# Sliding-window attention on one core: head order across banks, and value products one clip later

## What is computed

```python
h0 = the 125 x 128 tokens of a clip; x = layernorm(h0)
qkv = (x @ W_qkv + b_qkv).reshape(B, S, 3, HEADS, HD)      # S = 125
q, k, v = ...                                              # per head
scores[s, o] = q[s] . k[s + o] * scale    for o in -32..32, inside the clip
attn = softmax(scores) @ v(shifted)
z = attn @ W_proj + b_proj + h0
out = z + (z - mean(z)) / sqrt(var(z) + 1e-5)              # per token
```

## Time and profile before

| what | value |
|---|---|
| runs | median 547.76 us (547.48 to 548.02, 3 runs) |
| the profiled execution | 550.68 us, its span 548.9 us |
| busy over the span | PE 92%, DVE 74%, ACT 65%, POOL 60% |
| 420 to 450 us (window loop) | PE 28.99 of 30 us, DVE 26.90, ACT 25.55, POOL 17.50, granted clock 1.00 |
| 400 to 410 us | PE 9.48 of 10 us, granted clock 0.75 |
| 540 us to the end | PE 1.74 of 9 us |

### The profile page before, as it was taken

How to read it: one execution, slowest core, us unless ns; L and a number is a source line. 1 busy time by engine, 2 the same in 40 slices (tenths; PEclk the granted TensorE clock), 3 DMA queues, 4 the chain that set the end, 5 groups by cost and what they waited for, 6 DMA issues and landing times.

```text
span 548.9 us, 13987 instructions
## 1 busy us (share of the span) xinstructions
PE 503.3 (92%) x4554; PEld 355.3 (65%) x4554; DVE 408.9 (74%) x1728; ACT 358.4 (65%) x1072; POOL 329.2 (60%) x367
## 2 busy tenths in 40 slices
PE   6998899999998599999999999997599999999983
PEld 4778666666665357766667776655367766776762
DVE  3797757888886367787877777865369988898993
ACT  5985558889887244454455445453578888888881
POOL 2860647778886556776666676663126555565654
PEclk9999559999999699999999999999779999999997
DMA  4440212222222010000000000000000000000000
GB/s 163 138 161 11 64 34 51 56 62 62 63 60 75 20 37 20 19 20 22 35 22 20 19 20 20 1 1 1 0 2 2 20 21 20 13 11 21 20 21 20
DMA packets 21946, 19.89 MB, mean 36 GB/s; under 512 B 14210, under 2 KB 18466, under 8 KB 21746
## 3 DMA queue, kind: packets, MB, share of 16 engines
q1 hardware_dynamic: 21298, 18.28, 11.6%
q10 hardware_dynamic: 576, 0.71, 0.4%
HBM read 16.81 MB, written 2.18 MB: 35 GB/s over the span
## 4 chain that ended last, share of the span: by engine, by line
PE 44%; DVE 15%; issue 4%; ACT 2%; POOL 2%; POOLq 0%; DVEq 0%; ACTq 0%
PE quad L802 10%; PE quad L779 9%; PE bank L824 6%; PE bank L888 4%; PE bank L899 4%; DVE quad L1156 4%; PE bank L905 3%; PE quad L771 2%; PE bank L880 2%; DVE z_all L1186 2%; DVE otok L1168 2%; DVE st_all L1188 2%; DVE wmax L1156 2%; PE bank L793 1%; PE bank L817 1%
## 5 line engine op out<-in xcount | busy, mean ns | idle before, releaser
L476 POOL TENSOR_SCALAR put<-keyb,c 100x1000 f32<-100x1000 bf16 x32 | 89.0, 2782 | 47.9 <-DMA keyb<-key_scratch 26.3
L972 ACT ACTIVATE wprobs<-quad,wmax 125x125 f32<-125x125 f32 x256 | 75.5, 372 | 19.7 <-DVE wmax L1156 19.7
L1156 DVE CUSTOM_DVE_ANT_0 quad<-quad,c 125x125 f32<-125x125 f32 x256 | 66.1, 311 | 9.1 <-PE quad L847 9.1
L609 ACT ACTIVATE probs<-quad,negmax 100x250 f32<-100x250 f32 x128 | 58.3, 467 | 21.8 <-DVE negmax L561 20.9
L779 PE MATMUL quad<-h1T,w 128*128 128x500 f32 x128 | 61.9, 609 | 0.7 <-ACT hid L943 0.6
L802 PE MATMUL quad<-w,hid 128*125 128x128 f32 x512 | 58.8, 273 | 0.1
L802 PEld LDWEIGHTS quad<-w,hid 128*125 128x125 f32 x512 | 57.3, 188 | 0.8 <-issue 0.5
L1058 POOL TENSOR_TENSOR kbd<-wkT,c 128x250 f32<-128x250 f32 x32 | 19.2, 600 | 53.0 <-ACT wkT L980 53.0
L491 PE MATMUL bank<-c,probs 100*125 100x100 f32 x256 | 48.3, 316 | 2.2 <-ACT probs L609 1.4
L491 PEld LDWEIGHTS bank<-c,probs 100*125 100x125 f32 x256 | 36.8, 209 | 20.6 <-issue 13.2
L943 ACT ACTIVATE hid<-quad,vec_cols 128x500 f32<-128x500 f32 x64 | 43.0, 675 | 7.4 <-PE quad L779 4.1
(11 more groups left out here) (131 smaller groups left out, 1267.9 us busy)
## 6 DMA issues: line engine op xcount, KB each, us to landing
keyb<-key_scratch SPq DMA_DIRECT2D x64, 97.7 KB
xa<-xT SPq DMA_DIRECT2D x8, 500.0 KB, 3.6
xt<-xtok SPq DMA_DIRECT2D x16, 250.0 KB
out<-o_all SPq DMA_DIRECT2D x7, 250.0 KB
w<-weights SPq DMA_DIRECT2D x1, 1024.0 KB, 7.2
vec_rows<-rows SPq DMA_DIRECT2D x1, 448.0 KB, 5.2
c<-consts ACTq DMA_DIRECT2D x1, 428.5 KB, 6.5
w<-weights ACTq DMA_DIRECT2D x1, 192.0 KB, 4.2
```

The lines of the kernel that those rows point to most:

```text
L476: nc.gpsimd.tensor_scalar(put[u % 3][:, :, :], keyb[p][:, :, :], c[0:ROWS, CONST["sidx"]], None, ALU.is_equal).then_inc(put_done, 1)
L609: nc.scalar.activation(probs[p][:, ch, :], s_bank[ch][0:ROWS, 0:L], ACT.Exp, bias=negmax[p][:, ch:ch + 1], accum_out=rowsum[p][:, ch:ch + ...
L972: ins = nc.scalar.activation(probs[p][:, j, :], s_of(j), ACT.Exp, bias=negmax[p][:, j:j + 1], scale=-1.0)
L1156: ins = nc.vector.tensor_tensor_reduce(s_of(j), s_of(j), c[0:LH, CONST["band"]], 1.0, OFF, ALU.add, ALU.min, negmax[p][:, j:j + 1])
```

## The change

- The heads are taken in the order 0, 2, 4, 6, 1, 3, 5, 7, so that neighbours in the order lie in different banks. Every minimum and every exponential has its own signal and wait; a minimum from the fifth on waits for the exponential that read the same bank.
- VectorE: two minima, L1165 and L1168, four minima, L1176, two minima, then L1186 (z), then the copy L1181, then L1188 and L1192.
- ScalarE: L980, then L991, L982, L986, two exponentials, L999, six exponentials.
- TensorE: scores, then the output transposes (L863), then L857, L871, then the value products (L899), now of clip u-2, then L876, L880, L888, L905.
- Everything behind the products (L863, L880, L905, z, statistics, last scaling) belongs to clip u-3 instead of u-2 (GpSimd: u-4 instead of u-3); the values have three buffers instead of two; every engine gets one more drain call. y_of and y_proj move within the bank.

```diff
@@ -696,7 +696,7 @@
...
 kbd = pair("kbd_", [128, 2, LH])
-vo = pair("vo_", [LH, H, CW])
+vo = [sb(f"vo_{i}", [LH, H, CW]) for i in range(3)]
 negmax = pair("wmax_", [LH, H])
@@ -723,7 +723,8 @@
...
 x_k, x_q, x_v = x_bank[:, 0:LH], x_bank[:, 128:128 + LH], x_bank[0:LH, 256:256 + D]
-y_a, y_of, y_proj = y_bank[0:LH, 256:512], y_bank[:, 0:LH], y_bank[0:LH, 256:256 + D]
+y_a, y_of, y_proj = y_bank[0:LH, 256:512], y_bank[:, 256:256 + LH], y_bank[0:LH, 384:384 + D]
+ORDER = (0, 2, 4, 6, 1, 3, 5, 7)
@@ -826,7 +827,7 @@
...
-    pe.wait_ge(ones_in, 2)
+    pe.wait_ge(ones_in, 3)
@@ -842,26 +843,26 @@
...
             pe.wait_ge(kbd_done, u + 1)
-            wait(pe, exp_done, 4 * u)
+            wait(pe, exp_done, H * u)
             for cc in range(4):
...
+        if within(u, 3, B + 3):
+            pe.wait_ge(oT_done, u - 2)
+            for i in range(2):
+                ins = nc.tensor.transpose(y_a[:, 128 * i:128 * i + 128], oT[:, LH * i:LH * i + LH], ident)
+            ins.then_inc(otok_ready, 1)
         if within(u, 1, B + 1):
-            pe.wait_ge(exp_done, 4 * u)
+            pe.wait_ge(exp_done, H * u)
             wait(pe, pT1_done, u - 1)
...
             for j in range(4):
-                ins = nc.tensor.transpose(t_bank[1][0:LH, LH * j:LH * j + LH], probs[pm][:, 4 + j, :], ident[0:LH, 0:LH])
+                ins = nc.tensor.transpose(t_bank[1][0:LH, LH * j:LH * j + LH], probs[pm][:, ORDER[4 + j], :], ident[0:LH, 0:LH])
             ins.then_inc(pT1_ready, 1)
-        if within(u, 2, B + 2):
-            pe.wait_ge(oT_done, u - 1)
-            for i in range(2):
-                ins = nc.tensor.transpose(y_a[:, 128 * i:128 * i + 128], oT[:, LH * i:LH * i + LH], ident)
-            ins.then_inc(otok_ready, 1)
@@ -870,42 +871,44 @@
...
             ins.then_inc(qk_ready, 1)
+        if within(u, 2, B + 2):
+            wait(pe, otok_done, u - 2)
+            wait(pe, oT_done, u - 2)
+            pe.wait_ge(pT0_done, u - 1)
+            pe.wait_ge(pT1_done, u - 1)
+            pe.wait_ge(v_done, u - 1)
+            if u == 2:
+                pe.wait_ge(n3T_done, NP)
+            for j in range(H):
+                ins = nc.tensor.matmul(y_bank[CW * (j % 4):CW * (j % 4) + CW, LH * (j // 4):LH * (j // 4) + LH],
+                                       vo[(u - 2) % 3][:, ORDER[j], :], probsT[p][:, j, :], start=True, stop=True)
+            ins.then_inc(pv_ready, 1)
         if within(u, -1, B - 1):
...
-        if within(u, 2, B + 2):
-            pe.wait_ge(otok_done, u - 1)
+        if within(u, 3, B + 3):
+            pe.wait_ge(otok_done, u - 2)
             nc.tensor.transpose(y_of, otok[:, :], ident[0:LH, 0:LH]).then_inc(oF_ready, 1)
...
         if within(u, 0, B):
-            pe.wait_ge(exp_done, 4 * u + 2)
+            pe.wait_ge(exp_done, H * u + 4)
             wait(pe, pT0_done, u)
...
             for j in range(4):
-                ins = nc.tensor.transpose(t_bank[0][0:LH, LH * j:LH * j + LH], probs[p][:, j, :], ident[0:LH, 0:LH])
+                ins = nc.tensor.transpose(t_bank[0][0:LH, LH * j:LH * j + LH], probs[p][:, ORDER[j], :], ident[0:LH, 0:LH])
             ins.then_inc(pT0_ready, 1)
...
-        if within(u, 1, B + 1):
-            wait(pe, oF_done, u - 1)
-            pe.wait_ge(pT0_done, u)
-            pe.wait_ge(pT1_done, u)
-            pe.wait_ge(v_done, u)
-            if u == 1:
-                pe.wait_ge(n3T_done, NP)
-            for j in range(H):
-                ins = nc.tensor.matmul(y_bank[CW * (j % 4):CW * (j % 4) + CW, LH * (j // 4):LH * (j // 4) + LH],
-                                       vo[pm][:, j, :], probsT[pm][:, j, :], start=True, stop=True)
-            ins.then_inc(pv_ready, 1)
-        if within(u, 2, B + 2):
-            pe.wait_ge(oF_done, u - 1)
+        if within(u, 3, B + 3):
+            pe.wait_ge(oF_done, u - 2)
             nc.tensor.matmul(y_proj, oF[:, :], w[:, WEIGHT["wp"]], start=True, stop=True).then_inc(proj_ready, 1)
...
     in_turn(pe, ffn, window)
-    for u in range(B, B + 2):
+    for u in range(B, B + 3):
         at(window, u)
@@ -965,12 +968,12 @@
...
-        def exponents(cc):
-            act.wait_ge(min_done, 4 * u + cc + 1)
-            for j in range(2 * cc, 2 * cc + 2):
-                ins = nc.scalar.activation(probs[p][:, j, :], s_of(j), ACT.Exp, bias=negmax[p][:, j:j + 1], scale=-1.0)
-            ins.then_inc(exp_done, 1)
+        def exponents(lo, hi):
+            for k in range(lo, hi):
+                j = ORDER[k]
+                act.wait_ge(min_done, H * u + k + 1)
+                nc.scalar.activation(probs[p][:, j, :], s_of(j), ACT.Exp, bias=negmax[p][:, j:j + 1], scale=-1.0).then_inc(exp_done, 1)
@@ -978,32 +981,31 @@
...
             nc.scalar.activation(kT[:, :], x_k, ACT.Identity, bias=col("wk_b")).then_inc(kT_done, 1)
+        if within(u, 3, B + 3):
+            act.wait_ge(pv_ready, u - 2)
+            wait(act, otok_ready, u - 3)
+            wait(act, z_done, u - 3)
+            nc.scalar.activation(oT[:, :], y_bank[:, 0:2 * LH], ACT.Copy).then_inc(oT_done, 1)
+        if within(u, -1, B - 1):
             wait(act, scores, u)
...
             act.wait_ge(v_ready, u + 1)
-            wait(act, pv_ready, u - 1)
-            nc.scalar.activation(vo[p][:, :, 0:HD], x_v.rearrange("p (h f) -> p h f", h=H), ACT.Copy).then_inc(v_done, 1)
-        if within(u, 2, B + 2):
-            act.wait_ge(pv_ready, u - 1)
-            wait(act, otok_ready, u - 2)
-            wait(act, z_done, u - 2)
-            nc.scalar.activation(oT[:, :], y_bank[:, 0:2 * LH], ACT.Copy).then_inc(oT_done, 1)
+            wait(act, pv_ready, u - 2)
+            nc.scalar.activation(vo[u % 3][:, :, 0:HD], x_v.rearrange("p (h f) -> p h f", h=H), ACT.Copy).then_inc(v_done, 1)
         if within(u, 0, B):
             wait(act, pT0_ready, u - 1)
-            exponents(0)
-            exponents(1)
+            exponents(0, 2)
         if within(u, 1, B + 1):
...
         if within(u, 0, B):
-            exponents(2)
-            exponents(3)
+            exponents(2, 8)
...
     in_turn(act, ffn, window)
-    at(window, B)
-    at(window, B + 1)
+    for u in range(B, B + 3):
+        at(window, u)
@@ -1058,8 +1060,8 @@
...
-        if within(u, 3, B + 3):
-            b = u - 3
+        if within(u, 4, B + 4):
+            b = u - 4
             pool.wait_ge(mean_done, b + 1)
@@ -1071,7 +1073,7 @@
...
     in_turn(pool, ffn, window)
-    for u in range(B, B + 3):
+    for u in range(B, B + 4):
         at(window, u)
@@ -1141,58 +1143,59 @@
...
-    for i in range(2):
+    for i in range(3):
         nc.vector.memset(vo[i][:, :, HD:CW], 1.0).then_inc(ones_in, 1)
...
         u, _, _ = shift(h, p, 0)
-        um2, _, _ = shift(h, p, -2)
-        def mask_and_max(cc):
-            if cc == 0:
-                dve.wait_ge(scores, u + 1)
-            for j in range(2 * cc, 2 * cc + 2):
-                ins = nc.vector.tensor_tensor_reduce(s_of(j), s_of(j), c[0:LH, CONST["band"]], 1.0, OFF, ALU.add, ALU.min, negmax[p][:, j:j + 1])
-            ins.then_inc(min_done, 1)
-        if within(u, 0, B):
-            mask_and_max(0)
-            mask_and_max(1)
-        if within(u, 2, B + 2):
-            dve.wait_ge(otok_ready, u - 1)
-            wait(dve, otok_done, u - 2)
+        b = u - 3
+        def mask_and_min(lo, hi):
+            for k in range(lo, hi):
+                j = ORDER[k]
+                if k >= 4:
+                    dve.wait_ge(exp_done, H * u + k - 3)
+                nc.vector.tensor_tensor_reduce(s_of(j), s_of(j), c[0:LH, CONST["band"]], 1.0, OFF, ALU.add, ALU.min,
+                                               negmax[p][:, j:j + 1]).then_inc(min_done, 1)
+        if within(u, 0, B):
+            dve.wait_ge(scores, u + 1)
+            mask_and_min(0, 2)
+        if within(u, 3, B + 3):
+            dve.wait_ge(otok_ready, b + 1)
             nc.vector.reciprocal(rinv[:, :], y_a.rearrange("p (h f) -> p h f", h=H)[:, :, HD]).then_inc(rinv_done, 1)
-            dve.wait_ge(rinv_done, u - 1)
-            wait(dve, oF_ready, u - 2)
-            nc.vector.tensor_tensor(otok[:, :].rearrange("p (h f) -> p h f", h=H),
-                                    y_a.rearrange("p (h f) -> p h f", h=H)[:, :, 0:HD],
-                                    rinv[:, :].unsqueeze(2).to_broadcast([LH, H, HD]), ALU.mult).then_inc(otok_done, 1)
-        if within(u, 0, B):
-            mask_and_max(2)
-        if within(u, 2, B + 2):
-            dve.wait_ge(oF_ready, u - 1)
-            wait(dve, proj_ready, u - 2)
+            dve.wait_ge(rinv_done, b + 1)
+            wait(dve, oF_ready, b)
+            nc.vector.tensor_tensor(otok[:, :].rearrange("p (k c f) -> p c k f", k=4, c=2),
+                                    y_a.rearrange("p (c k f) -> p c k f", c=2, k=4)[:, :, :, 0:HD],
+                                    rinv[:, :].rearrange("p (c k) -> p c k", c=2).unsqueeze(3).to_broadcast([LH, 2, 4, HD]),
```

(31 more changed lines are left out.)

## The result

The changed kernel takes 555.29 us in the median (554.29 to 557.6, 4 runs) against 547.62 us of the kernel before; the ratio is 1.0151 with a 95% interval of 1.0114 to 1.0188, so it is 7.7 us slower where 5.7 was forecast. That is only 4.4 above the profiled execution of before (550.68), because this one reached the loop earlier.

A forecast was written before the change was run, and what follows sets the result against it. A circle through TensorE, VectorE and ScalarE was taken to bound the kernel. Its period going from 4.37 to 4.50 us adds 3.6 over 28 periods; head -1.3, drain +3.4: +5.7 on 547.76 gives 553.5 us, range 547.6 to 558.0.

The forecast's parts named there:

- The new wait: VectorE at L1176 (oF): ready at 1.82 after the first minimum, held by L880 until 2.34, half a microsecond.
- The second circle: From oF through last two minima, last exponentials and scores: next first minimum at 4.50, between 4.45 and 4.63.
- The first circle: VectorE behind oF: z at 3.27, copy no longer hidden, to 4.07, statistics and next minimum 0.43: period 4.50.
- B: Circle named after the measurement: first minimum, four exponentials, first transposes, projection, z, copy, statistics, next first minimum.
- The order of heads and the signals: ScalarE: first exponential at 0.42 instead of 0.67 after the first minimum, 0.25 earlier; signal and wait per head cost nothing.
- the faster rival: Minima and exponentials: alternating banks frees accesses that hold each other; period 4.15 to 4.2, 545.1 us; chance 0.11.
- The rule of the Trainium skill: VectorE operations start only once the pipe is empty: z and copy 0.97 instead of 0.80, period 4.67; forecast kept the rows.
- The head: Loop start: scores of clip 2 come 0.9 earlier, its call bounded by ScalarE 0.4 shorter; together -1.3 us.
- The drain: Loop end: one more call without scores, a further z 3.80 later with nothing covering it; +3.4 us.
- The sum: Whole kernel: periods +3.6, head -1.3, drain +3.4, together +5.7 us, giving 553.5 us.
- the rivals: Period stays, 549.9 us (0.13); no measurable change, 547.9 (0.10); faster, 545.1 (0.11); slower still, 559.1 (0.11).

The follow-up runs named there:

- values_late: Changed kernel with the values' matmuls moved from between the products and L895 to behind the projection; 549.47 us, ratio 1.0020 to the kernel before.
- heads_only: Kernel before with only the new order of heads and a signal and wait per minimum and exponential; 541.66 us, ratio 0.9882.
- later_only: Changed kernel with heads in natural order and minima and exponentials signalled in pairs, products still one clip later; 562.16 us, ratio 1.0247 to the kernel before.
- copy_first: Changed kernel with VectorE's copy of the transposed exponentials put back ahead of z; 559.26 us, ratio 1.0227 to the kernel before.
- minima_first: Changed kernel with oF put behind the last two minima on VectorE, copy still behind z; 553.21 us, ratio 1.0104 to the kernel before.
- both_first: Changed kernel with oF behind the last two minima and the copy ahead of z; 551.66 us, ratio 1.0059 to the kernel before.

## Why the prediction was right, point by point

**The new wait.** Forecast: products and values ahead of L895 (named L880 then) keep oF until 2.34 after the first minimum. Measured 2.37, with a wait of 0.38 at nearly every clip. Two small errors cancel in part: L895 starts at 2.05 instead of 1.97, but lasts 0.27 instead of 0.33. values_late shows that this stretch sets the period: 0.32 less there, 0.25 less in the period.

**The second circle**, through oF, minima, exponentials and scores, was put at 4.50; it is the one that sets the period, 4.53. Its term for the handover from the last exponential to the scores, 0.08 between 0.06 and 0.15, was too small: 472.12 + 0.62 to 472.88 is 0.14.

**The first circle**, z and the exposed copy, was also put at 4.50, and here a step failed, though the number did not. The sum timed L880 from the scores, 0.78 ahead of a first minimum that they release, and then let copy and statistics release the next one. That is a path from the scores to the next first minimum, and no circle. It is there: z at 3.29 and 1.21 more make 4.50, and the scores release that minimum 0.03 later. That both sums came to 4.50 was luck. B, which does close, is 4.27 in values_late, so the copy behind z is not the price of the change; moved ahead of z, alone, it makes the kernel slower by 0.09 a period. That L988 waits for z and that there is room for it was right for the order forecast: it ends 0.25 ahead of L855.

**The order of heads and the signals.** Forecast were 0.25 for the earlier first exponential and nothing for the signals. In heads_only the period is 0.24 shorter, 0.19 of it by the earlier transposes, and the exponentials keep their pace. That accesses to one bank by one engine hold each other (the faster rival) is excluded by the same rows: 1.13 for four exponentials in either order.

**The rule of the Trainium skill** ("VectorE: DVE Perf Modes", section on the DRAIN), by which z and copy would take 0.97: z to copy is 0.21, copy to statistics 0.58, together 0.79, so they do not take 0.97. The section itself adds that "A next op that is not held starts earlier", which the forecast had left out; these rows, between which VectorE waits for no other engine, are in line with that. The rule's second half, that a semaphore costs nothing extra, agrees with heads_only.

**The head** was put at -1.3 and is -0.8. The -0.9 ahead of the scores of clip 2 came as -0.8 (5.29 us from the scores of clip 1 instead of 6.12); the -0.4 behind them did not come. The call of clip 2 was costed with a distance of 0.78 from scores to first minimum, a distance at full clock. It was 1.28 (400.43 to 401.71): the granted clock was 0.57 of full speed between 400 and 402 us, and L848 took 1.21 instead of 0.70.

**The drain** was put at +3.4 and is +4.0. The z are 3.80, 4.32 and 4.00 apart, where the forecast had added one 3.80 to the distances of before, 3.80 and 3.69. In the last two TensorE works at the lower of its two levels: the granted clock was 0.58 between 541 and 545 us and 0.50 from 545 to 550, after a stretch, 536 to 541, in which TensorE was busy 2.78 of 5 us. There L895 lasts 0.47 instead of 0.33 and L908 and L855 0.79 instead of 0.48, which makes 0.5 and 0.3 more for these two z. The first z of the drain comes 3.82 after the last scores instead of 4.05, which gives 0.2 back.

**The sum**, 5.7 against 7.7: 0.9 of the difference in the periods, 0.5 in the head, 0.6 in the drain. The 5.7 falls short by a quarter, and the copy, to which the text gave the price, is not what sets the period; the wait that it had for the cause, oF behind the products, is. None of the rivals came.

## What to carry to other kernels

When a step is moved earlier on an in-order engine, list what now stands behind it and who waits for that: here the products left the stretch between the exponentials and z, and entered the one ahead of oF, behind which VectorE's last minima were queued. Of a change with two parts, run each alone: the order of heads with its signals gains 6 us, which the move of the products hid by losing twice that. When a period is added up from a chain, check that the chain closes: what releases its first step must be what its last step releases. A pipeline one clip deeper costs its extra pass through the drain, at the pace and the clock of the drain.

## What the runs showed of the hardware

- Signalling and waiting per head on VectorE and ScalarE took no time that shows: minima about 0.245 us apart and exponentials 0.25 apart, with one signal for each or for two.
- The distance between the same two TensorE steps depends on what else the second waits for. The projection starts 0.53 to 0.54 behind four transposes and takes 0.38 where oF ended 0.18 us or more ahead of it (values_late, later_only). Where it starts 0.05 to 0.06 after the end of oF, it is 0.60 to 0.62 behind the transposes and takes 0.48 (the changed kernel, copy_first, minima_first, both_first).
